# Cross attention on one core: the query product and the transposed sums of another pair share one turn of the PSUM ring

## The reference

```
xn = layer_norm(x, g1, b1)
ln_lat = layer_norm(latents, g2, b2)
q = ln_lat @ Wq
kv = jnp.concatenate([xn, ln_lat], axis=1) @ Wkv
...
weight = jnp.einsum('bhld,bhnd->bhln', q * scale, k * scale)
weight = jnp.where(full_mask[:, None, None, :], weight, neg)
weight = jax.nn.softmax(weight.astype(jnp.float32), axis=-1).astype(q.dtype)
out = jnp.einsum('bhln,bhnd->bhld', weight, v)
...
return out @ Wout
```

## Time and profile before

| | |
|---|---|
| median of three runs | 1154.55 us (1153.27 to 1154.87) |
| the profiled execution, its own time | 1154.32 us |
| its span in the profile | 1152.5 us |
| TensorE matmuls busy | 1104.0 us (96%) |
| TensorE weight loads busy | 946.9 us (82%) |
| VectorE, ScalarE, GpSimd busy | 879.1, 735.5, 539.6 us |

### The profile page before, as it was taken

How to read it: one execution, slowest core, us unless ns; L and a number is a source line. 1 busy time by engine, 2 the same in 40 slices (tenths; PEclk the granted TensorE clock), 3 DMA queues, 4 the chain that set the end, 5 groups by cost and what they waited for, 6 DMA issues and landing times. The chain is left out here.

```text
span 1152.5 us, 27526 instructions
## 1 busy us (share of the span) xinstructions
PE 1104.0 (96%) x8781; PEld 946.9 (82%) x8781; DVE 879.1 (76%) x2786; ACT 735.5 (64%) x1754; POOL 539.6 (47%) x892
## 2 busy tenths in 40 slices
PE   6999997999999999999999999999999998999997
PEld 5888875778888887887888888888788887999997
DVE  7999996888878788778787878877878685655554
ACT  6999996667757666666765766666667565322221
POOL 4666665554574355446456445544644432400101
PEclk9999999999999999999999999999999999999999
DMA  2000011000000000000000000000000003000000
GB/s 92 7 7 11 7 44 38 1 11 1 2 1 11 2 1 11 1 1 11 2 1 1 11 2 1 2 1 2 1 2 1 2 1 96 3 10 6 11 6 11
DMA packets 14685, 12.39 MB, mean 11 GB/s; under 512 B 1361, under 2 KB 13649, under 8 KB 14417
## 3 DMA queue, kind: packets, MB, share of 16 engines
q1 hardware_dynamic: 14128, 10.43, 3.0%
q10 hardware_dynamic: 416, 0.20, 0.1%
HBM read 9.57 MB, written 1.05 MB: 9 GB/s over the span
## 5 line engine op out<-in xcount | busy, mean ns | idle before, releaser
L874 POOL TENSOR_TENSOR xk_parts<-k_raw,xk_parts 64x768 fp32r<-64x768 f32 x128 | 236.1, 1845 | 312.7 <-DVE xk_parts L992 310.0
L1016 DVE CUSTOM_DVE_ANT_0 xmasked<-ps,bar 128x768 f32<-128x768 f32 x256 | 244.3, 954 | 4.2 <-issue 0.6
L1128 PE MATMUL ps<-xk_parts,xq_parts 128*128 128x512 f32 (+1 forms) x1024 | 233.2, 350 | 6.9 <-DVE xq_parts L997 3.4
L929 ACT ACTIVATE xprobs<-xmasked,xlow 128x768 f32<-128x768 f32 x256 | 238.0, 930 | 1.4 <-DVE xlow L1016 1.4
L1134 PE MATMUL ps<-ident,xprobs 128*128 128x128 f32 x1536 | 215.0, 276 | 7.1 <-DVE xlow L1016 6.0
L1128 PEld LDWEIGHTS ps<-xk_parts,xq_parts 128*128 128x128 f32 x1024 | 174.4, 189 | 33.3 <-DVE xq_parts L997 3.8
L1134 PEld LDWEIGHTS ps<-ident,xprobs 128*128 128x128 f32 x1536 | 168.9, 140 | 16.7 <-DVE xlow L1016 10.8
L1145 PE MATMUL ps<-xprobs_t,xvals 128*64 128x256 f32 x1536 | 179.9, 383 | 1.1 <-ACT xprobs_t L935 1.1
L1145 PEld LDWEIGHTS ps<-xprobs_t,xvals 128*64 128x64 f32 x1536 | 104.8, 137 | 57.9 <-issue 10.6
L1021 DVE COPY xprobs_t<-ps 128x768 f32<-128x768 f32 x128 | 121.6, 950 | 3.5 <-PE ps L1134 3.5
L909 ACT ACTIVATE k_raw<-ps 128x768 f32<-128x768 f32 x64 | 52.0, 812 | 105.1 <-PE ps L1102 94.3
(11 more groups left out here) (220 smaller groups left out, 2524.8 us busy)
## 6 DMA issues: line engine op xcount, KB each, us to landing
ctx_in<-in_ctx SPq DMA_DIRECT2D x8, 256.0 KB, 3.3
w_rest<-in_L_ffn_w SPq DMA_DIRECT2D x2, 768.0 KB, 6.4
raw_kv<-in_L_xattn_Wkv SPq DMA_DIRECT2D x1, 1024.0 KB, 5.3
out<-state SPq DMA_DIRECT2D x8, 128.0 KB, 2.0
x_in<-in_x SPq DMA_DIRECT2D x7, 128.0 KB, 2.2
raw_q<-in_L_xattn_Wq SPq DMA_DIRECT2D x1, 512.0 KB, 6.1
wout<-in_L_xattn_Wout SPq DMA_DIRECT2D x1, 512.0 KB, 3.9
keep_all<-in_mask_BxS_bk SPq DMA_DIRECT2D x1, 512.0 KB, 4.7
```

The costliest lines, as they stand in the source:

```text
L874: pool.tensor_tensor(k_parts[dst, i // 2 % 2, h, :], k_raw[src, :], k_parts[src, i // 2 % 2, h, :].bitcast(F32), ALU.subtract).then_inc(k_ ...
L929: nc.scalar.activation(probs[:, i % 4, :], masked[:, i % 4, :], ACT.Exp, scale=-1.0, bias=low[:, i % 4:i % 4 + 1], accum_out=sums[:, pair ...
L1016: dve.tensor_tensor_reduce(masked[:, i % 4, :], slot(slots.place("S", i), KEYS), bar[:, par, :], 1.0, 3e38, ALU.add, ALU.min, low[:, i % 4 ...
L1128: last = nc.tensor.matmul(slot(s, hi - lo, lo), q_parts[:, pair % 2, h, part, t * P:(t + 1) * P], k_parts[:, pair % 2, h, lo:hi], start=pa ...
```

## The change

Q and R no longer have a turn each. The transposes of R now go to the second bank of the place whose first bank Q fills, in the same turn of TensorE: Q of pair i is followed at once by R of pair i-3. A batch has 91 turns in place of 99. The place is free when both VectorE's low part of the queries and ScalarE's copy of the sums are done. Since 91 is no multiple of three, the place of a step now depends on the batch too. For the shared turn Q moves behind PT and PV, to where R stood; on ScalarE Q's two copies move behind the PT copy, and on VectorE Q's low part moves behind HI. After the last batch the step "Q" comes three more times for R alone. The rest of the diff passes the batch to `place` and `has`.

```diff
-    def has(self, kind, batch):
-
-        return 0 <= batch < self.batches + (kind in self.beyond)
+    def has(self, kind, batch, i):
+
+        return 0 <= batch < self.batches or batch == self.batches and i < self.beyond.get(kind, 0)
...
-    def place(self, kind, i):
-        return (self.at[kind, i] + self.shift) % self.places
+    def place(self, kind, i, batch=0):
+        n = self.at[kind, i]
+        return ((batch - self.mine[n][1]) * len(self.mine) + n + self.shift) % self.places
...
-    full = {k: sem(f"x_{k}_full") for k in ("TC", "TX", "K", "Q", "V", "S", "PT", "R", "OUT")}
+    full = {k: sem(f"x_{k}_full") for k in ("TC", "TX", "K", "Q", "V", "S", "PT", "OUT")}
+    r_full = sem("x_R_full")
...
+        if kind == "Q" and batch < B:
+            return q_lo_done, batch * XH + 2 * i + 2
         if kind == "Q":
-            return q_lo_done, batch * XH + 2 * i + 2
+            rb, ri = r_of(batch, i)
+            return rsum_t_ready, rb * PAIRS + ri + 1
...
+    R_LATER = 3
+
+    def r_of(b, i):
+
+        return (b, i - R_LATER) if i >= R_LATER else (b - 1, i - R_LATER + PAIRS)
+
     pe_order = Order(B, UNITS, {
-        "S": (UNITS, -2.25), "K": (PAIRS, -5.75), "Q": (PAIRS, -7.25), "V": (PAIRS, -4),
-        "R": (PAIRS, 5.25), "PV": (PAIRS, 5), "PT": (UNITS, 0.75), "OUT": (1, 37.75),
-        "TC": (1, -13), "TX": (1, -14.5)}, beyond=("TX", "TC"))
+        "S": (UNITS, -2.25), "K": (PAIRS, -5.75), "Q": (PAIRS, -6.75), "V": (PAIRS, -4),
+        "PV": (PAIRS, 5), "PT": (UNITS, 0.75), "OUT": (1, 37.75),
+        "TC": (1, -13), "TX": (1, -14.5)}, beyond={"TX": 1, "TC": 1, "Q": R_LATER})
...
-        "S": (UNITS, -1.75), "Q": (PAIRS, -6), "HI": (XH, -4), "RECIP": (PAIRS, 2.5),
+        "S": (UNITS, -1.75), "Q": (PAIRS, -5.9), "HI": (XH, -4), "RECIP": (PAIRS, 2.5),
...
-        "K": (PAIRS, -5), "Q": (PAIRS, -6.75), "V": (PAIRS, -3.25), "R": (PAIRS, 5.5),
-        "PT": (UNITS // 2, 1.25), "EXP": (UNITS, -1), "TC": (1, -12.5), "TX": (1, -14)}, beyond=("TX",))
+        "K": (PAIRS, -5), "Q": (PAIRS, -6.6), "V": (PAIRS, -3.25), "R": (PAIRS, 5.5),
+        "PT": (UNITS // 2, 1.25), "EXP": (UNITS, -1), "TC": (1, -12.5), "TX": (1, -14)}, beyond={"TX": 1})
...
-                act.wait_ge(full["R"], b * PAIRS + i + 1)
+                act.wait_ge(r_full, b * PAIRS + i + 1)
                 wait(act, heads_ready, b * PAIRS + i - 1)
-                nc.scalar.activation(rsum_t[:, i % 2, :], slot(slots.place("R", i), S), ACT.Copy).then_inc(rsum_t_ready, 1)
+                nc.scalar.activation(rsum_t[:, i % 2, :], slot(slots.place("Q", (i + R_LATER) % PAIRS, b + (i + R_LATER) // PAIRS), S, BANK), ACT.Copy).then_inc(rsum_t_ready, 1)
...
+                    if earlier[0] == "Q" and earlier[1] < B:
+                        rb, ri = r_of(*earlier[1:])
+                        wait(pe, rsum_t_ready, rb * PAIRS + ri + 1)
...
-            if kind == "Q":
+            if kind == "Q" and b < B:
...
-            if kind == "R":
-                pe.wait_ge(wide_ready, b * PAIRS + i + 1)
-                for j in range(T):
-                    last = nc.tensor.transpose(slot(s, P, j * P),
-                                               rsum_wide[:, i % 2, j, :, :].rearrange("p h c -> p (h c)"), ident[:, :])
-                last.then_inc(full["R"], 1)
+            if kind == "Q" and r_of(b, i)[0] >= 0:
+                rb, ri = r_of(b, i)
+                pe.wait_ge(wide_ready, rb * PAIRS + ri + 1)
+                for j in range(T):
+                    last = nc.tensor.transpose(slot(s, P, BANK + j * P),
+                                               rsum_wide[:, ri % 2, j, :, :].rearrange("p h c -> p (h c)"), ident[:, :])
+                last.then_inc(r_full, 1)
```

More of the change, by code:

```diff
@@ L78, in run @@
                 b = w + rel
-                if self.has(kind, b) and not (w == -1 and kind in done) and (kind, b) not in left and (kind, b, i) not in left:
+                if self.has(kind, b, i) and not (w == -1 and kind in done) and (kind, b) not in left and (kind, b, i) not in left:
                     emit(kind, b, b % 2, i)
@@ L105, in before @@
             batch = batch + (rel2 - rel - (n < self.places))
-            if self.order.has(kind, batch):
+            if self.order.has(kind, batch, i):
                 return kind, batch, i
@@ L882, in emit @@
                 pool.wait_ge(rsum_ready, n + 1)
-                wait(pool, full["R"], n - 1)
+                wait(pool, r_full, n - 1)
                 for j in range(T):
@@ L914, in emit @@
                     rows = slice(h * XD, (h + 1) * XD)
-                    nc.scalar.activation(q_parts[rows, i % 2, h, 0, :], slot(slots.place("Q", i), S)[rows, :],
+                    nc.scalar.activation(q_parts[rows, i % 2, h, 0, :], slot(slots.place("Q", i, b), S)[rows, :],
                                          ACT.Copy, scale=Q_SCALE).then_inc(q_hi_done, 1)
@@ L997, in emit @@
                     dve.scalar_tensor_tensor(out=q_parts[rows, i % 2, h, 1, :],
-                                             in0=slot(slots.place("Q", i), S)[rows, :], scalar=Q_SCALE,
+                                             in0=slot(slots.place("Q", i, b), S)[rows, :], scalar=Q_SCALE,
                                              in1=q_parts[rows, i % 2, h, 0, :].bitcast(F32),
@@ L1039, in emit @@
                 tokens = state[:, bass.ds(b * T, T), :]
-                dve.tensor_tensor(tokens, slot(slots.place("OUT", 0), T * D).rearrange("p (t d) -> p t d", t=T), tokens,
+                dve.tensor_tensor(tokens, slot(slots.place("OUT", 0, b), T * D).rearrange("p (t d) -> p t d", t=T), tokens,
                                   ALU.add).then_inc(added, 1)
@@ L1067, in emit @@
             if kind in full:
-                s = slots.place(kind, i)
+                s = slots.place(kind, i, b)
                 earlier = slots.before(kind, b, i)
@@ L1091, in emit @@
                 last.then_inc(full[kind], 1)
-            if kind in ("K", "Q", "V"):
+            if kind in ("K", "V") or kind == "Q" and b < B:
                 pe.wait_ge(m.cross_hi, 3 * B)
@@ L1187, in cross_attention @@
     c.pe_order, c.dve_order, c.act_order, c.pool_order = pe_order, dve_order, act_order, pool_order
-    c.free = slots.place("OUT", 0) + 2
+    c.free = slots.place("OUT", 0, B - 1) + 2
     c.transposed, c.summed, c.done = (full["PT"], B * UNITS), (pv_done, B * PAIRS), (added, B)
@@ L1192, in last_user @@
     def last_user(s):
-        uses = [(B - 1 + (k in pe_order.beyond), rel, at, k, i) for at, (k, rel, i) in enumerate(slots.mine)
-                if slots.place(k, i) == s]
-        b, _, _, kind, i = max(uses, key=lambda u: (u[0] - u[1], u[2]))
+        _, _, b, kind, i = max((b - rel, at, b, k, i) for at, (k, rel, i) in enumerate(slots.mine) for b in range(B - 2, B + 1)
+                               if pe_order.has(k, b, i) and slots.place(k, i, b) == s)
         return taken(kind, b, i)
```

21 lines of the change are left out of this document (10 added, 11 removed).

## The result

The changed kernel takes 1174.37 us, the median of 4 runs (1173.48 to 1175.1). The kernel before took 1154.71 us in 4 runs beside it (1153.27 to 1155.07). The ratio is 1.0175, 95% interval 1.016 to 1.0189: 1.75% slower. The profiled execution took 1173.48 us, its span is 1171.7 us and the granted clock 0.997. That is 19.2 us more than the profiled execution of before; I had worked out 15.1 us.

The account below looks back on a forecast made before the run. TensorE's chain and VectorE's slackless work up to the last PT were taken as the bound. Losses of 10.0 + 1.1 + 0.4 + 3.6 = 15.1 us gave 1169.4 us (likeliest case 1165.7 to 1171.9; stated range 1152 to 1176).

Parts of the forecast that it names:

- likeliest case: Whole kernel: the later first reduction makes it slower, 1169.4 us (1165.7 to 1171.9), chance 0.72.
- The first reduction: VectorE, plain groups: starts 0.25 us later (0.19 to 0.29) behind Q's low part; 10.0 us in 40 groups.
- those that begin a batch: Groups where a batch begins: the reduction already starts 0.10 us later, so 0.15 us lost in 7 groups, 1.1 us.
- The groups with OUT: VectorE's wait for the output product swallows the delay; only TensorE's 0.05 us is left in 7 groups, 0.4 us.
- The 0.05 us that I added for Q behind PV: TensorE: Q behind PV costs 0.00 to 0.10 us more a group; the middle, 0.05 us, was taken.
- without slack: VectorE, first reduction to last PT: 3.43 us of work without slack, so a later reduction delays the next group equally.
- K: K's start stays in time or waits for 0.1 us, which the later reduction covers.
- the turns saved remove none of the waits that I see: TensorE's order of places: the eight turns saved per batch remove no visible wait.
- The rival in which the shared turn holds K: K slips 0.3 us more than VectorE's delay in 47 groups, 14 us: about 1183 us, chance 0.10.
- The group with TX: ScalarE is the bound; copy of the sums, exponential, `y`, `xt` and K shift 0.45 us in 8 groups, 3.6 us.
- Hidden: Rival: the first reduction is not later, at most TensorE's 0.05 us is lost: 1154.3 to 1157 us, chance 0.10.
- Faster, the ring is short: Rival: PT's waits on VectorE, 10.8 us, go and the weight-load gap fills: 1144 to 1150 us, chance 0.08.

Follow-up runs that it names:

- experiment 3: Changed kernel, but from the second batch on the high and low parts of Q are made for only 64 of 256 queries: 1157.82 us, ratio 1.0036.
- experiment 2: Changed kernel with the shared turn at Q's old place, sums of four pairs before instead of three: 1151.25 us, ratio 0.9979 to the kernel before.
- Experiment 5: Changed kernel with both TWICE copies one reduction later on VectorE: 1181.87 us, ratio 1.0239 to the kernel before.
- experiment 1: Kernel before with Q moved as in the change, but Q and R keeping a turn each (99 a batch): 1186.16 us, ratio 1.0278.
- experiment 9: Shared turn at Q's old place, both TWICE copies joined directly behind the low part, ahead of HI: 1143.78 us, ratio 0.9905 to the kernel before.
- experiment 10: Kernel before with both TWICE copies joined behind the low part and ahead of HI: 1146.38 us, ratio 0.9929.
- experiment 7: Shared turn at Q's old place, both TWICE copies joined behind the low part and HI: 1163.52 us, ratio 1.0077 to the kernel before.
- experiment 8: Kernel before with both TWICE copies joined behind the low part and HI, nothing else changed: 1149.07 us, ratio 0.9956.

## Why the prediction was right, and by how much it was off

*That the kernel gets slower, and by what.* Right. The low part of Q has become the last thing ahead of the first reduction. Making it short removes the loss (experiment 3), and leaving Q at its old place removes it too (experiment 2).

*The number.* 1174.37 us lies 2.5 us above the likeliest case's own range (1165.7 to 1171.9). It lies inside the stated range of 1152 to 1176, whose upper end no term of the sum gives. That the range held is in part luck; the mechanism was right, its terms were too small. The signs in the profile say the same: the first reduction is 1.48 us behind its S (1.3 to 1.4 forecast), the last PT 0.34 us later (0.2 to 0.3), a plain group 0.31 us longer (0.25), and K in the group with TX 0.59 us later behind the first S (0.45). The last PT visibly waits for the accumulator read in nearly all plain groups and those that begin a batch, and in none with TX.

*The first reduction.* This is the term of the sum that was too small. I took 0.25 us a plain group, between 0.19 and 0.29; the groups lost 0.31. I had the low part's end at Q plus 1.95, and it is there (678.86 to 679.93 + 0.88 = 680.81). I had the reduction 0.04 us behind it; it came 0.13 us behind (680.94), so 2.08 us after Q. The 0.04 us was read behind TWICE, and there the memset costs no time of its own: the profile shows it beside the reduction (670.70, the reduction from 670.67). Behind the low part memset and reduction follow one after the other, as behind idle time: 0.07 us between their starts in both (668.19, 668.26). And my middle value leaned on the hope that Q runs as in mid-stream, although the gap behind PV that spoke against it was in the rows. The 40 plain groups account for 2.3 of the 4.0 us by which the sum was short, those that begin a batch for 0.4 (0.21 us each, not 0.15), those with TX for 0.9, and 0.6 us were lost ahead of the first group, for which I had no term. The groups with OUT gave 0.2 back.

*TensorE.* Q to first S is 0.60 us (678.86 to 679.46), as worked out. The 0.05 us that I added for Q behind PV is in it, but PV starts 0.06 us sooner behind its PT (0.75 us instead of 0.81), so that TensorE's part outside VectorE's chain comes out 0.03 us shorter than before. In the groups with OUT, where only this was to be left, 0.2 us in all was lost, not 0.4.

*From the first reduction to the last PT.* The forecast of "without slack" was right for the end, incomplete for the way: I named only the reduction of the second unit as holding TensorE. Experiment 5 showed the other link, the copy of a PT behind the first reduction, whose slack of 0.16 us was used up first.

*K.* In time, as forecast: 1.40 us behind the first S, 0.04 later than before. The rival in which the shared turn holds K does not occur. What I did not see is how it would be with Q in a turn of its own: the wait for the low part would have fallen on PT (experiment 1). I said that the turns saved remove none of the waits that I see; against the order before this holds; with Q in its new place they do remove one, worth 12 us.

*The group with TX.* Here 0.57 us instead of 0.45. ScalarE's copy of the sums starts 1.46 us after Q, where I had 1.34. TensorE and ScalarE in that group:

```profile
653.85 0.39 PE L1120 MATMUL ps<-y_hi,wq_hi 128*128 128x256 f32 x1
...
655.85 0.87 PE L1147 MATMUL ps<-ident,xprobs 128*128 128x128 f32 x6
...
657.39 0.50 PE L1113 MATMUL ps<-y_hi,wk_hi 128*128 128x512 f32 x1 [0.67 <-ACT xt L914]
```

```profile
654.50 0.78 ACT L925 ACTIVATE xq_parts<-ps 64x256 fp32r<-64x256 f32 x2 [2.48 <-PE ps L1122]
655.31 0.39 ACT L951 ACTIVATE xrsum_t<-ps 128x256 f32<-128x256 f32 x1
...
656.96 0.38 ACT L914 ACTIVATE xt<-ps 128x256 f32<-128x256 f32 x1
```

The copy of the sums follows Q's high part after 0.03 us, not 0.10 us ahead of its end. Here the PT behind the first S is the third turn after the shared one, so it starts 0.97 us behind its S (which starts at 654.88), 0.18 us more than in a plain group; I had overlooked that wait, and K's on ScalarE covers it.

*The rivals.* "Hidden" falls with the late reduction. "Faster, the ring is short" falls with experiment 2: with the low part early and 91 turns the PTs wait for VectorE nearly as long as before (9.1 us, 10.8). The Trainium skill (Perfetto Trace Analysis, Optimization Strategy) reads a gap that repeats on the saturated engine as a possible want of PSUM; here the repeating wait was formally for a PSUM place, and it went when VectorE's chain got shorter (to 2.8 us in 6 places in experiment 9, to none in experiment 10). The runs do not bear this rule out for this kernel.

## What to carry to other kernels

When an operation moves into another engine's idle time, ask where in that idle time its input arrives: at the end of it, it delays whatever the idle time was waiting for, and here 0.31 us in each of 40 groups made 12.3 of the 19 us. A wait for a buffer place names the ring, but its cure may be the reader of the buffer; follow what stands ahead of that reader on its engine, link by link, since the first link without slack decides. Before filling VectorE's idle time with copies, look at what GpSimd does in the same stretch.

## What the runs showed of the hardware

A copy of 64x512 from SBUF to SBUF on VectorE takes 0.42 us. While GpSimd works on LO (64x768, 1.83 us), such a copy waits. In experiment 7 all 57 copies that start during a LO, 0.04 to 0.35 us into it, last 1.75 to 2.07 us; in experiment 8 it is 50 copies with 1.93 to 2.05 us. Whenever in the LO they start, they end 0.28 to 0.29 us behind its end. So do copies that start late in one and last hardly longer than alone, as here in the kernel before (672.24 + 1.85 = 674.09, 673.88 + 0.49 = 674.37):

```profile
672.24 1.85 POOL L874 TENSOR_TENSOR xk_parts<-k_raw,xk_parts 64x768 fp32r<-64x768 f32 x1 [4.36 <-DVE xk_parts L992]
673.88 0.49 DVE L1006 CAST xq_parts<-xq_parts 64x512 fp32r<-64x512 f32 x1
```

With the order exchanged, so that LO starts behind the copies, their mean is back at 0.44 us. The profile shows this wait as a long operation, not as idle time. HI, too, is a copy within SBUF (0.55 us); in the changed kernel one that starts 0.34 us into a LO lasts 2.06 us.

That agrees with the Trainium skill (SBUF, State Buffer, the section on SBUF's two separate sides): VectorE in a mode that uses two ports and GpSimd share one pair of ports, the one that comes second waits for the whole instruction of the other. The reductions and the PT copies, which read PSUM, stayed at 0.94 to 0.96 us beside GpSimd in all of these runs, and the low part, which reads PSUM too, at no more than 0.43 us. No run here varied the copy's mode by itself, so that the ports are the cause rests on the page; that the copies wait while GpSimd works on LO, and that exchanging the order removes it, is what the runs show. GpSimd's `xrsum_wide`, `y_lo` and `cxt_lo` (the 0.79 us row of experiment 7) make copies longer in the same way, but not every operation of GpSimd does. A copy that starts inside a root of 128x2 ends before it, after its usual 0.42 us:

```profile
625.86 0.69 POOL L831 TENSOR_TENSOR r_root<-r_var,x_powers 128x2 f32<-128x2 f32 x1
626.08 0.42 DVE L1006 CAST xq_parts<-xq_parts 64x512 fp32r<-64x512 f32 x1
```

By the rule above this copy, too, would have waited; here the measurement decides, and why it did not wait is open.
